# Pair sums added by DMAs from the GpSimd queue, and output products cut into quarters, in a windowed attention

## What is computed

```
q = Wq @ x + bq ; k = Wk @ cond + bk ; v = Wv @ cond + bv      # x, cond: (B, 64, 512)
k, v padded along T, then windows of W = 16 columns: k_win, v_win (B, H, hd, T, W)
dots = einsum('bhdt,bhdtw->bhtw', qh, k_win) * hd ** -0.5       # 8 heads
attn = softmax(dots, axis=-1)
out  = einsum('bhtw,bhdtw->bhdt', attn, v_win)
x    = x + (Wo @ out + bo)
```

## Time and profile before

| | us |
|---|---|
| median of 3 runs | 1657.7 |
| lowest and highest | 1657.53, 1663.36 |
| the profiled execution | 1665.81 |
| its span | 1664.5 |
| stage of 64 steps: first wide product to first instruction of the last add to x | 119.87 to 237.21 |
| TensorE, VectorE, GpSimd busy in the whole span | 1598.4, 1007.3, 570.7 |

### The profile page before, as it was taken

One profiled execution on the slowest core, in us unless ns is written; L12 is line 12 of the kernel. 1 busy time (PEld: TensorE's weight loads), 2 busy tenths in 40 slices (PEclk: granted clock), 3 DMA queues, 4 the chain that ended last, 5 costly groups with the idle time before them and its releaser, 6 DMA issues.

```text
span 1664.5 us, 22246 instructions
## 1 busy us (share of the span) xinstructions
PE 1598.4 (96%) x9380; PEld 1153.3 (69%) x9380; DVE 1007.3 (61%) x1328; ACT 470.1 (28%) x682; POOL 570.7 (34%) x402
## 2 busy tenths in 40 slices
PE   8979989999989999999999999999999999899998
PEld 2264447888648877888887888878755466568886
DVE  5987765222562666564556556565661389787665
ACT  4140012000432324232433323342111456630010
POOL 3907643221155424232423313141141054462221
PEclk9989979999999999999999999999999999999999
DMA  3000022100200121011010110100300021500000
GB/s 129 1 1 0 1 95 108 35 17 33 101 13 1 38 88 42 24 63 39 26 38 26 64 31 34 39 1 1 150 4 8 19 54 28 195 1 13 14 13 14
DMA packets 18019, 66.55 MB, mean 40 GB/s; under 512 B 1440, under 2 KB 9760, under 8 KB 13312
## 3 DMA queue, kind: packets, MB, share of 16 engines
q1 hardware_dynamic: 17920, 65.12, 11.3%
HBM read 58.82 MB, written 2.10 MB: 37 GB/s over the span
## 4 chain that ended last, share of the span: by engine, by line
PE 84%; DVE 11%; issue 2%; ACT 1%; POOL 1%; DMA 1%; SPq 0%; DVEq 0%; ACTq 0%; POOLq 0%
PE banks L270 47%; PE banks L264 30%; PE banks L399 2%; DVE arena L442 2%; PE banks L1920 1%; PE banks L1324 1%; PE banks L2193 1%; DVE arena L234 1%; DVE window L483 1%; DVE window L420 1%; DMA arena<-in_x 1%; ACT dense L2054 1%; DVE window_split L459 1%; PE banks L283 1%; DVE window L455 0%
## 5 line engine op out<-in xcount | busy, mean ns | idle before, releaser
L270 PE MATMUL banks<-grouped_split 128*128 128x512 f32 x1536 | 367.8, 394 | 1.8 <-DVE grouped_split L1470 1.2
L270 PEld LDWEIGHTS banks<-grouped_split 128*128 128x128 f32 x1536 | 283.1, 188 | 66.4 <-issue 6.3
L1610 POOL TENSOR_TENSOR arena<-arena,attn_tables 128x512 f32<-128x512 f32 x80 | 102.2, 1282 | 298.9 <-ACT arena L1544 298.9
L270 PE MATMUL banks<-experts_split 128*128 128x512 f32 (+1 forms) x792 | 181.7, 392 | 1.9 <-DVE experts_split L630 1.9
L270 PEld LDWEIGHTS banks<-experts_split 128*128 128x128 f32 (+1 forms) x792 | 146.5, 185 | 36.4 <-issue 2.5
L1425 DVE TENSOR_TENSOR arena<-banks,attn_tables 128x512 f32<-128x512 f32 x80 | 54.6, 684 | 112.4 <-ACT arena L1544 111.9
L264 PE MATMUL banks<-arena 128*128 128x64 f32 (+2 forms) x698 | 109.5, 308 | 8.2 <-DMA arena<-in_c 6.4
L264 PEld LDWEIGHTS banks<-arena 128*128 128x128 f32 x698 | 95.3, 192 | 27.6 <-issue 18.5
L660 DVE SCALAR_TENSOR_TENSOR arena<-banks,experts,arena 128x512 f32<-128x512 f32 x64 | 47.6, 749 | 106.8 <-PE banks L270 106.8
L1438 DVE TENSOR_TENSOR arena<-arena 128x512 f32<-128x512 f32 x80 | 73.1, 915 | 57.2 <-POOL arena L1610 56.3
L509 POOL TENSOR_TENSOR window<-window 128x1024 f32<-128x1024 f32 x32 | 75.6, 2367 | 74.0 <-DVE window L483 73.8
(11 more groups left out here) (289 smaller groups left out, 2974.3 us busy)
## 6 DMA issues: line engine op xcount, KB each, us to landing
grouped<-in_attn SPq DMA_DIRECT2D x16, 1024.0 KB, 5.1
experts<-in_expert SPq DMA_DIRECT2D x8, 1024.0 KB, 4.8
linear<-in_ffn SPq DMA_DIRECT2D x1, 4096.0 KB, 13.4
grouped<-in_attn SPq DMA_DIRECT2D x8, 512.0 KB, 3.6
dense<-arena SPq DMA_DIRECT2D x16, 256.0 KB, 4.7
dense<-in_w SPq DMA_DIRECT2D x1, 3584.0 KB, 12.1
dense<-in_attn SPq DMA_DIRECT2D x1, 3072.0 KB, 13.6
dense<-in_w SPq DMA_DIRECT2D x1, 2688.0 KB, 10.0
```

What stands on the lines that cost most here:

```text
L270: s = pe.matmul(dst, lhsT=lhsT[i], rhs=rhs[j], start=(k == 0 and x == 0), stop=(k == n - 1 and x == 2))
L1610: g_.tensor_tensor(rot, rot, SIN[:, h * HALF:(h + 1) * HALF], ALU.mult).then_inc(rot_sin.sem, 1)
```

## The change

Three things are changed in the stage of 64 steps.

1. **Fours.** After every second pair sum, the first 15 times, GpSimd starts a DMA from its own queue that adds the newer pair sum into the older one (`accum_op=ALU.add`, 128 x 1024 float32, 512 KB, SBUF to SBUF). It waits first for its own pair sum. The landing raises one of four semaphores `fours`. The products with Wo are then made once for four steps, not once for two: 15 fours and the last two pair sums as they are. In place of 8 slots there are 16, in three places in memory (`slots_of_products` deals them out; former[n] is the step whose data lay in the slot, and VectorE waits for whoever read it last).
2. **Quarters.** The output products are 256 columns wide. A four's products are four such pieces (two tiles by two halves), and `quarter(q, x)` puts one into each step from 13 steps behind the four's first product on (`LAG`); two steps after the start of a pair of tiles carry two pieces each and the next two none. VectorE's two adds to x and its two measurements come apart, behind four different steps.
3. **Products of constants.** `stay_busy` before step 0 runs 27 times and no longer 22. One more product of constants stands in each of the first 13 steps, and in four steps of each 16 after that.

The diff, without lines that only declare names:

```diff
+def slots_of_products(free):
+    hold, until, last = (18, 8, 14, 8), [0] * len(free), [None] * len(free)
+    slots, former = [], []
+    for n in range(4 * WIN):
+        j = min(range(len(free)), key=lambda i: until[i])
+        assert until[j] <= n
+        slots.append(free[j])
+        former.append(last[j])
+        until[j], last[j] = n + hold[n % 4], n
+    return slots, former
...
-    AV, SLOTS, SUM = DOTS, 8, PROD + 2048
+    SUM, LAG = PROD + 2048, 13
+    slots, former = slots_of_products([at + j * 2 * D for at, n in ((DOTS, 8), (K0, 4), (XT, 4)) for j in range(n)])
...
+    def four_done(q):
+        return fours[q % 4](16 * (q // 4 + 1))
...
-        stay_busy(m, pe, 7, 22)
+        stay_busy(m, pe, 7, 27)
...
-        def to_out(k):
-            p = k // 8
-            pe.wait_ge(*pair_done(k + 1))
-            if k % 8 == 0 and p >= 2:
-                pe.wait_ge(*add_done(2 * (p - 1)))
-            for i in range(2):
-                s = mm(pe, bank[:, 4 + p % 2 * 2 + i, :], f(W0 + 3 * P, P), f(AV + (2 * k % SLOTS * 2 + i) * D, D),
-                       k % 8, 8)
-            s.then_inc(out_mm.sem, 1)
+        def to_out(p, n, i, h, first, last):
+            return pe.matmul(bank[:, 4 + p % 2 * 2 + i, h * 256:(h + 1) * 256], lhsT=f(W0 + 3 * P, P),
+                             rhs=f(slots[n] + i * D + h * 256, 256), start=first and h == 0, stop=last and h == 1)
+        def quarter(q, x):
+            if x == 0:
+                pe.wait_ge(*four_done(q))
+                if q % 4 == 0 and q >= 8:
+                    pe.wait_ge(*add_done(2 * (q // 4 - 1)))
+            s = to_out(q // 4, 4 * q, x // 2, x % 2, q % 4 == 0, q % 4 == 3)
+            if x == 3:
+                s.then_inc(out_mm.sem, 1)
...
-            if n % 2 and n >= 5:
-                to_out((n - 5) // 2)
-        to_out(30)
-        to_out(31)
+            at, phase = (n - LAG) // WIN, (n - LAG) % WIN
+            q = (n - LAG) // 4
+            if at < 0:
+                stay_busy(m, pe, 4, 1)
+            elif phase < 2:
+                quarter(q, 2 * phase)
+                quarter(q, 2 * phase + 1)
+            elif phase >= 4:
+                quarter(q, phase % 4)
+            if at >= 0 and phase in (2, 3, 4, 6):
+                if at:
+                    pe.wait_ge(*add_done(2 * at))
+                stay_busy(m, pe, 4 + (at + 1) % 2 * 2, 1)
+        for q in (13, 14):
+            for x in range(4):
+                quarter(q, x)
+        for k in (30, 31):
+            pe.wait_ge(*pair_done(k + 1))
+            for x in range(4):
+                s = to_out(3, 2 * k, x // 2, x % 2, False, k == 31)
+        s.then_inc(out_mm.sem, 1)
...
-            if n >= SLOTS:
-                v.wait_ge(*out_mm((n - SLOTS) // 2 + 1))
+            if old is not None:
+                if old % 4 == 0:
+                    v.wait_ge(*out_mm(old // 4 + 1))
+                elif old % 4 == 2:
+                    v.wait_ge(*four_done(old // 4))
+                else:
+                    v.wait_ge(*pair_done(old // 2 + 1))
...
-            if w == 7 and p:
-                add(p - 1)
-        add(3)
+            at, phase = (n - LAG) // WIN, (n - LAG) % WIN
+            if at > 0:
+                if phase < 2:
+                    add(at - 1, phase)
+                elif phase in (4, 6):
+                    measure(at - 1, phase // 2 - 2)
+        measure(2, 0)
+        measure(2, 1)
+        add(3, 0)
+        add(3, 1)
+        measure(3, 0)
+        measure(3, 1)
...
-            g.tensor_tensor(f(at, 2 * D), f(at, 2 * D), f(at + 2 * D, 2 * D), ALU.add).then_inc(pair_done.sem, 1)
+            g.tensor_tensor(to, to, other, ALU.add).then_inc(pair_done.sem, 1)
+            if k % 2 and k < 30:
+                g.wait_ge(*pair_done(k + 1))
+                g.dma_start(f(slots[2 * k - 2], 2 * D), to, accum_op=ALU.add).then_inc(fours[k // 2 % 4].sem, 16)
             if k == 27:
                 m.rsqrt_half(g, 1, 0)
```

More of the change, by code:

```diff
@@ L309, in attn0 @@
     selt_done, wide_mm, av_done, pair_done, out_mm = (
-        m.sem(n, k) for n, k in (("selt_done", 1), ("wide_mm", 64), ("av_done", 64), ("pair_done", 32), ("out0_mm", 32)))
+        m.sem(n, k) for n, k in (("selt_done", 1), ("wide_mm", 64), ("av_done", 64), ("pair_done", 32), ("out0_mm", 16)))
+    fours = [m.sem(f"four_done{i}") for i in range(4)]
+    def four_done(q):
+        return fours[q % 4](16 * (q // 4 + 1))
     add_done = m.sem("add0_done", NT)
@@ L466, in vector, with add, measure @@
         low(3)
[L468 to L476, removed]
+        def add(p, i):
+            v.wait_ge(*out_mm(4 * (p + 1)))
+            x = f(X + PAIRS[p][i] * D, D)
+            v.scalar_tensor_tensor(x, bank[:, 4 + p % 2 * 2 + i, :], bias0[:, 3:4], x, ALU.add, ALU.add).then_inc(add_done.sem, 1)
+        def measure(p, i):
+            v.wait_ge(*add_done(2 * p + i + 1))
+            m.moments(v, 1, PAIRS[p][i])
         for n in range(4 * WIN):
-            p, w = n // WIN, n % WIN
+            p, w, old = n // WIN, n % WIN, former[n]
             v.wait_ge(*wide_mm(n + 1))
-            if n >= SLOTS:
-                v.wait_ge(*out_mm((n - SLOTS) // 2 + 1))
-            v.tensor_tensor(f(AV + n % SLOTS * 2 * D, 2 * D, 2, D), bank[:, n % 2 * 2:n % 2 * 2 + 2, :],
-                            spread(f(V0 + PAIRS[p][0] * KW + w, D), 2, 2 * KW, D), ALU.mult).then_inc(av_done.sem, 1)
-            if w == 7 and p:
-                add(p - 1)
-        add(3)
+            if old is not None:
[5 more added lines that the diff above has]
+                    v.wait_ge(*pair_done(old // 2 + 1))
+            v.tensor_tensor(f(slots[n], 2 * D, 2, D), bank[:, n % 2 * 2:n % 2 * 2 + 2, :],
+                            spread(f(V0 + PAIRS[p][0] * KW + w, D), 2, 2 * KW, D), ALU.mult).then_inc(av_done.sem, 1)
+            at, phase = (n - LAG) // WIN, (n - LAG) % WIN
[10 more added lines that the diff above has]
+        measure(3, 1)
     def pool(g):
@@ L506, in pool @@
         for k in range(2 * WIN):
-            at = AV + 2 * k % SLOTS * 2 * D
+            to, other = (f(slots[2 * k + x], 2 * D) for x in (0, 1))
             g.wait_ge(*av_done(2 * k + 2))
-            g.tensor_tensor(f(at, 2 * D), f(at, 2 * D), f(at + 2 * D, 2 * D), ALU.add).then_inc(pair_done.sem, 1)
+            g.tensor_tensor(to, to, other, ALU.add).then_inc(pair_done.sem, 1)
+            if k % 2 and k < 30:
+                g.wait_ge(*pair_done(k + 1))
+                g.dma_start(f(slots[2 * k - 2], 2 * D), to, accum_op=ALU.add).then_inc(fours[k // 2 % 4].sem, 16)
             if k == 27:
```

## The result

The changed kernel takes 1665.3 us (median of 20 runs) where the kernel before takes 1659.3 (20 runs): the medians are 6.0 us apart. The ratio of the two is 1.0028, interval 1.0016 to 1.0041, that is **4.6 us slower**; the interval belongs to the ratio, so the text goes by 4.6. The prediction said 1646, range 1637 to 1662.

What follows compares the result with a forecast made beforehand. TensorE was taken to bound the stage at 3.04 us for two steps; afterwards GpSimd's queue and the tail (217.8 + 5.3 + 2.5 = 225.6) end it 11.6 us earlier, so 1657.7 - 11.6 = 1646.1, said as 1646, range 1637 to 1662.

Steps and rivals of the forecast that it cites:

- What bounds the kernel: 64-step stage before the change: TensorE sets the pace at 3.04 us for two steps, plus start, tail and slow-clock stretches.
- the hole of 2.02 us: TensorE without a product ahead of step 0, followed by slow clock; five more products of constants were to cover it.
- TensorE's term: New step of four wide products and one short piece: 0.67 + 0.20 + 0.44 = 1.31 us; last VectorE product about 213.
- GpSimd's term: GpSimd's queue: 1.15 us for each of 15 DMAs, wait included; last pair sum ends at 217.5.
- Dear and cheap issue: Rivals on DMA issue price: cheap, 0.4 us, 1641, chance 0.17; dear, 1657 without gain (0.18) or 1669 slower (0.09).
- The tail: Stage end: last landing 5 us, at 217.8; then twelve short products 5.3 us, plus 2.5 for slow clock.
- The mark: Start of the stage's last add to x; forecast at 225.6 against 237.21 in the first trace before the change.
- with the adds dealt out I expect the clock at 1.00 through the steps: TensorE's granted clock stays at 1.00 through the 64 steps, adds to x and measurements being spread over different steps.
- The rival "the clock": TensorE falls to 1.2 GHz for whole stretches, 2.3 us a step, 32 us more over half the steps: 1678; chance 0.10.
- against 237.21: 11.6 us earlier: Last add to x starts at 225.6, not the first trace's 237.21; the whole 11.6 us carries to the end.
- The profiled execution's 8.1 us over the median: Baseline profiled execution of 1665.8 us stood 8.1 above the median 1657.7; the 11.6 us gain was subtracted from both.
- The range: Whole kernel: 1637 to 1662 us, leaving out the clock rival, most of dear issue and cheap issue's 22 us end.

Runs made afterwards that it cites:

- before_27: The kernel before with 27 products of constants ahead of step 0 and no longer 22; ratio 1.0001 to the kernel before.
- eps_no_const: after_act_eps without the products of constants inside the steps, the 27 ahead of step 0 kept; 1697.0 us, ratio 1.0219 to the kernel before.
- after_act_eps: The changed kernel with the one L239 addition in mid-stage moved from VectorE to ScalarE; 1656.9 us, ratio 0.9963 to the kernel before.
- after_again: The changed kernel, unedited, run for a second trace; 1665.9 us.
- before_again: The kernel before, unedited, run for a second trace; 1658.1 us.
- before_probe: The kernel before with extra small VectorE instructions, results unread, each placed behind a statistic while a GpSimd pair sum runs; no whole-run time given.
- after: The changed kernel as first measured; median 1665.3 us, its first trace from an execution of 1661.2 us.
- after_fill: The changed kernel with ten products of constants put on TensorE behind step 53's output piece; 1655.0 us, ratio 0.9954 to the kernel before.
- before: The kernel before the change as first measured; median 1659.3 us, its first trace from an execution of 1665.8 us.

## Why the prediction was wrong

**What bounds the kernel.** Right: TensorE at 3.04 us for two steps. The start was not: the hole of 2.02 us was named as what the slow clock follows, and before_27 shows that the clock falls with the hole closed. The products of constants inside the steps keep it up (eps_no_const). The five ahead of them do not do it alone; whether they are needed was not tested.

**TensorE's term.** 1.31 us a step forecast, 1.30 measured; VectorE's last product in after_act_eps near 210 against 213.

**GpSimd's term.** 1.15 for a DMA forecast, 1.16 measured; last pair sum 217.8 in after_act_eps (212.91 + 4.93) against 217.5. The prediction took its value from the shortest instruction that GpSimd had, so that it fits to 0.01 us is luck. With the 1 us of the Trainium skill (page "DMA: Bandwidth & Descriptors", section "Latency and other measured facts"), which is the time to the first byte, the sum gave 215.2, 2.6 us too early. Dear and cheap issue both fall.

**The tail.** Landing 5 forecast, 4.5 measured; slow clock in the last twelve products 2.5 forecast, 3.0 measured (8.34 - 5.3). The mark, 225.6 forecast, is 225.15 once L239 is out of the way. That it agrees to 0.5 us is partly luck: the landing came 1.0 us before its forecast, and the twelve products took 0.5 us longer.

**The step that failed first: "with the adds dealt out I expect the clock at 1.00 through the steps".** It did not hold: the granted clock is 0.50 from 201 to 227 us. The adds and measurements were costed, the measurements at 0.83 us each by the earlier trace rows, but L239 behind the fourth of them was put at nothing, without a reason. In the kernel before GpSimd has run dry when L239 comes, and it takes 0.17 us. In the changed kernel GpSimd is not dry there, because the DMAs put it behind; L239 takes 4.8 us, TensorE idles for 4.5 and the clock falls. The rival "the clock" had the price of a fallen clock right (1.0 us a step, here for twelve steps), but for its trigger it knew only thin steps and pauses of a few tenths, and had 0.10. Together it is 9.3 us, between 225.15 and the 234.45 of after_again (7.8 by the first trace, 232.98).

**The second: "against 237.21: 11.6 us earlier".** The baseline was one execution, and in this very stage it lay 5.8 us above before_again, whose time is near the median. The profiled execution's 8.1 us over the median was noted and then used as if it lay outside the stage. From 231.4 the same sum gives 5.8 us, and after_act_eps shows 6.3 at the mark. So 11.6 - 5.8 - 9.3 = -3.5, a loss; the two second traces show a loss of 3.0 at the mark, and the half microsecond between is that of the forecast mark. The rest of the measured 4.6 us lies behind the mark, where the traces drift apart by 1.5 to 4.8 us more; what causes that was not tested.

**The range** reached to 1662 by the issue price alone and so missed 1665.

## What to carry to other kernels

When a change puts an engine behind, look up every small instruction that used to fall into its idle time: here VectorE's instructions with two SBUF inputs, or a constant and one, waited for the sum that GpSimd was running. Look for the longest case of such an instruction in the whole trace, not only in the stage. A stall of TensorE is to be priced by the clock that follows and by whether the work behind it can bring the clock back, not by its own length; filling the hole with products of constants did as much here as removing it. And take the baseline of a stage from two traces before subtracting from it.

## What the runs showed of the hardware

- 0.17 us became 2.0 us beside one pair sum (before_probe) and 4.8 to 5.1 us beside two back to back (after, after_again, after_fill). Beside two shorter instructions back to back it got in between them in some traces (1.03 us in before_again) and not in others (2.25 us in before).
- TensorE stayed at 1.2 GHz (granted clock 0.50) through 24 us in which its records leave no gap in the changed kernel, and through 120 us with 117 busy in eps_no_const. What brings the clock back was not measured beyond the two step shapes.
- An accumulating SBUF-to-SBUF DMA of 512 KB from GpSimd's queue costs that queue 1.16 us, its own wait included, and lands 4.5 us after issue.
